# A vision-tower kernel: fewer token groups projected in front of the software pipeline, more inside it, and the column means taken from the scaled gains

## The reference, cut to what matters

```
p = layernorm(patches) * g1 + b1            # over 768
h = layernorm(p @ W_tok) * g2 + b2          # 768 -> 192
q, k, v = h @ W_qkv                         # 8 heads of 24
attn = softmax(normalised(q)^T normalised(k) * temp)   # 24 x 24 per head and image
h1 = layernorm(h + (attn v) @ W_proj + b_proj)
out = layernorm(h1 + soft_moe(h1))          # 8 experts, 4 slots each
```

## Time and profile before

| quantity | value |
|---|---|
| median of 3 runs | 140.48 us (139.16 to 142.77) |
| the profiled execution | 140.0 us, span 138.0 us |
| TensorE busy | 115.0 us (83%) |
| VectorE busy | 88.9 us (64%) |
| ScalarE busy | 69.0 us (50%) |
| GpSimd busy | 67.0 us (49%) |
| bytes moved | 10.34 MB in 7677 packets |

### The profile page before, as it was taken

How to read it: one execution, slowest core, us unless ns; L and a number is a source line. 1 busy time by engine, 2 the same in 40 slices (tenths; PEclk the granted TensorE clock), 3 DMA queues, 4 the chain that set the end, 5 groups by cost and what they waited for, 6 DMA issues and landing times.

```text
span 138.0 us, 4819 instructions
## 1 busy us (share of the span) xinstructions
PE 115.0 (83%) x1779; PEld 93.6 (68%) x1779; DVE 88.9 (64%) x380; ACT 69.0 (50%) x234; POOL 67.0 (49%) x158
## 2 busy tenths in 40 slices
PE   0297799999699999999999999997986860999920
PEld 0297799888377868578787796866964630788700
DVE  0211999999643687985857558586987440159980
ACT  3000004242862848648675686846644468763553
POOL 8500277767847428837265382743664000007871
PEclk9999999999999999999999999999999555599995
DMA  1999899988000000000000000000000000000232
GB/s 14 337 293 278 269 305 320 314 319 214 5 7 0 5 0 7 5 0 7 0 5 5 0 5 0 10 5 0 5 0 7 0 0 0 5 0 24 72 89 71
DMA packets 7677, 10.34 MB, mean 75 GB/s; under 512 B 2056, under 2 KB 5032, under 8 KB 7656
## 3 DMA queue, kind: packets, MB, share of 16 engines
q1 hardware_dynamic: 7656, 10.06, 24.2%
HBM read 9.17 MB, written 0.88 MB: 73 GB/s over the span
## 4 chain that ended last, share of the span: by engine, by line
PE 47%; DVE 22%; issue 12%; POOL 10%; ACT 4%; DMA 3%; SPq 1%; POOLq 1%; DVEq 0%; ACTq 0%
DVE st L649 8%; PE ps L565 7%; PE ps L436 6%; PE ps L476 5%; PE ps L496 3%; PE ps L542 3%; PE ps L399 3%; DMA wt<-in_w_tok 3%; PE ps L489 3%; PE ps L519 3%; DVE y L663 3%; PE ps L578 3%; DVE st L671 2%; PE ps L507 2%; PE ps L407 2%
## 5 line engine op out<-in xcount | busy, mean ns | idle before, releaser
L417 PE MATMUL ps<-wc,xT 128*108 128x192 f32 (+1 forms) x132 | 23.0, 327 | 1.5 <-DVE wc L637 1.5
L940 ACT ACTIVATE hT<-ps,b,g 96x108 f32<-96x108 f32 (+1 forms) x22 | 8.4, 430 | 27.9 <-PE ps L426 27.9
L417 PEld LDWEIGHTS ps<-wc,xT 128*108 128x108 f32 (+1 forms) x132 | 20.7, 170 | 2.0 <-DVE wc L637 1.8
L436 PE MATMUL ps<-wqk,hT 96*108 96x384 f32 (+1 forms) x44 | 16.2, 490 | 0.7 <-ACT qp L962 0.7
L1125 POOL TENSOR_SCALAR pw<-mv 108x1 f32<-108x1 f32 (+1 forms) x11 | 3.7, 337 | 21.3 <-DVE mv L780 21.3
L476 PE MATMUL ps<-hT,wv 96*128 96x108 f32 (+1 forms) x88 | 12.5, 284 | 0.0
L1139 POOL TENSOR_SCALAR var<-mv 108x1 f32<-108x1 f32 (+1 forms) x11 | 2.4, 223 | 18.9 <-DVE mv L875 18.4
L950 ACT ACTIVATE sq<-ps 108x384 f32<-108x384 f32 (+1 forms) x11 | 5.4, 490 | 12.4 <-PE ps L436 12.4
L476 PEld LDWEIGHTS ps<-hT,wv 96*128 96x128 f32 x88 | 10.7, 191 | 0.7
L649 DVE BATCH_NORM_STATS2 st<-xs 108x6 f32<-108x384 f32 (+1 forms) x22 | 10.9, 540 | 0.2 <-issue 0.2
L960 ACT ACTIVATE km<-ps,imgsel 108x192 f32<-108x192 f32 (+1 forms) x32 | 11.0, 418 | 0.0
(11 more groups left out here) (106 smaller groups left out, 304.6 us busy)
## 6 DMA issues: line engine op xcount, KB each, us to landing
xT<-in_x_t SPq DMA_DIRECT2D x10, 324.0 KB, 7.0
xs<-in_x SPq DMA_DIRECT2D x10, 324.0 KB
out<-o SPq DMA_DIRECT2D x10, 81.0 KB
wt<-in_w_tok SPq DMA_DIRECT2D x1, 576.0 KB, 4.2
wqk<-in_w_qk SPq DMA_DIRECT2D x1, 288.0 KB, 8.7
xT<-in_x_t SPq DMA_DIRECT2D x1, 216.0 KB, 7.5
xs<-in_x SPq DMA_DIRECT2D x1, 216.0 KB
wv<-in_w_v SPq DMA_DIRECT2D x1, 192.0 KB, 9.0
```

The costliest lines, as they stand in the source:

```text
L417: mm = pe.matmul(tokp(g), xT[:, o + kc * n:o + (kc + 1) * n], wc[:, kc, :], start=kc == 0, stop=kc == KC - 1)
L436: mm = pe.matmul(qkp(g), hT[:, f, t0:t0 + tokens(g)], wqk[:, f, :, :, :].rearrange("p j h d -> p (j h d)"), start=f == 0, stop=f == 1)
L940: ins = act.activation(hT[:, f, t0:t0 + tokens(g)], htp(g)[:, f, :], ACT.Identity, bias=b2[:, f:f + 1], scale=g2[:, f:f + 1])
```

## The change

The column means are taken directly from the weight: the multiplier is now `gs1`, the gains divided by 768, instead of a constant, so they no longer wait for `wg`. `wg` and `share` disappear. `wc` is formed in six slices, and the first projection goes on slice by slice. `offset` moves behind the projection of group 0, and its copy on VectorE behind the statistics of group 0. The gains and the biases come in one transfer, the weight in two, laid out so that each partition's part is contiguous.

`P1` becomes 3: three groups are projected in front of the loop (their two later turns in steps 0 and 1), the others in steps 0 to 5: two each in steps 0 and 1, one each in 2 to 5. Their turns follow two steps later. The group's vector and GpSimd stages move with them. The slots' loads move in front of the x loads from group 4 on, `slot_sums` into VectorE's step 1, `slot_scale` to step 3. Group 10's projection uses bank 7. Unchanged parts and the moved norms on GpSimd are left out of this cut of the diff where the description says it all:

```diff
-P1 = 9
+P1 = 3
+TOKENS = {0: (3, 4), 1: (5, 6), 2: (7,), 3: (8,), 4: (9,), 5: (10,)}
+def late(stage, s, i):
+    groups = TOKENS.get(s, ())
+    if i < len(groups):
+        stage(groups[i])
+def turn_step(g):
+    return 2 + next((t for t, groups in TOKENS.items() if g in groups), g - P1 - 1)
+def turned(s):
+    return P1 + sum(len(TOKENS.get(t, ())) for t in range(s - 1))
...
-            return ps[0:tokens(g), 6 + g % 2, 0:D]
+            return ps[0:tokens(g), 6 + g % 2 if g < NG - 1 else 7, 0:D]
...
-            sp.dma_start(g1[:, :], ln1_g).then_inc(ln1_in, 16)
-            sp.dma_start(b1[:, :], ln1_b).then_inc(ln1_in, 16)
-            sp.dma_start(wt[:, :, :], w_tok.rearrange("(k p) e -> p k e", p=128)).then_inc(wtok_in, 16)
+            sp.dma_start(gb1[:, :, :].rearrange("p t k -> p (t k)"), ln1_gb).then_inc(ln1_in, 16)
+            for i in range(2):
+                k0 = i * KC // 2
+                sp.dma_start(wt[:, k0:k0 + KC // 2, :].rearrange("p k e -> p (k e)"),
+                             w_tok[:, k0 * D:(k0 + KC // 2) * D]).then_inc(wtok_in[i], 16)
...
+            def column_means():
+                pe.wait_ge(gs1_ready, 1)
+                for kc in range(KC):
+                    if kc % (KC // 2) == 0:
+                        pe.wait_ge(wtok_in[kc // (KC // 2)], 16)
+                    mm = pe.matmul(csp(), gs1[:, kc:kc + 1].broadcast_to([128, 128]), wt[:, kc, :],
+                                   start=kc == 0, stop=kc == KC - 1)
+                mm.then_inc(csp_ready, 1)
...
                 if g >= 2:
-                    pe.wait_ge(y1_ready, g - 1)
+                    pe.wait_ge(y1_ready, g - 1 if g < NG - 1 else g)
                 for kc in range(KC):
+                    if g == 0:
+                        pe.wait_ge(wc_ready, kc + 1)
...
             def turn_h(g):
                 pe.wait_ge(n_ready, g + 1)
+                if turn_step(g) > 4:
+                    pe.wait_ge(xnT_ready, turn_step(g) - 4)
...
-            offset()
             column_means()
-            pe.wait_ge(wc_ready, 1)
             for g in range(P1):
                 token(g)
+                if g == 0:
+                    offset()
...
-                at(turn_h, s + P1 - 2 - 1, P1 - 2)
-                at(token, s + P1 - 1, P1)
+                if s < P1 - 1:
+                    turn_h(s + 1)
+                late(turn_h, s - 2, 0)
+                late(token, s, 0)
                 at(gram, s - 1)
                 at(mix, s - 2)
+                late(turn_h, s - 2, 1)
                 at(turn_xn, s - 4)
                 at(slot_in, s - 6)
                 at(norms, s)
+                late(token, s, 1)
...
+                for kc in range(KC):
+                    dve.scalar_tensor_tensor(wc[:, kc, :], wt[:, kc, :], gb1[:, 0, kc:kc + 1], csp(),
+                                             ALU.mult, ALU.subtract).then_inc(wc_ready, 1)
...
+            mean_shares()
             token_weights()
             x_stats(0)
             x_moments(0)
+            token_offset()
...
+                late(x_stats, s + 1, 0)
                 at(max_c, s - 5)
+                late(token_stats, s - 1, 0)
                 at(unit_h1, s - 4)
                 at(max_d, s - 5)
+                late(token_moments, s - 1, 0)
                 at(scales, s - 1)
+                late(x_moments, s + 1, 0)
                 at(y_sums, s - 2)
                 at(scores, s - 1)
+                late(token_out, s, 0)
+                late(token_stats, s - 1, 1)
...
+                late(x_moments, s + 1, 1)
                 at(take_d, s - 5)
-                at(ln2_norm, s + P1 - 2, P1)
+                late(ln2_norm, s - 1, 0)
+                late(ln2_norm, s - 1, 1)
                 at(residual_moments, s - 2)
+                late(token_out, s, 1)
```

More of the change, by code:

```diff
@@ L62, in tokens, with build @@
     return images(g) * TOK
-def build(nc, x, x_t, w_tok, ln1_g, ln1_b, ln2_g, ln2_b, g2col, b2col, w_qk, w_v, w_proj, b_proj, temp, slots, scale,
+def build(nc, x, x_t, w_tok, ln1_gb, ln2_g, ln2_b, g2col, b2col, w_qk, w_v, w_proj, b_proj, temp, slots, scale,
           w_down, b_down, w_up, b_up, ident_h, imgsel_h, negmask_h, out):
@@ L78, in build @@
         negmask = sb("negmask", [128, GI * SL])
-        g1 = sb("g1", [128, KC])
-        b1 = sb("b1", [128, KC])
+        gb1 = sb("gb1", [128, 2, KC])
+        gs1 = sb("gs1", [128, KC])
         wt = sb("wt", [128, KC, D])
-        wg = sb("wg", [128, KC, D])
         wc = sb("wc", [128, KC, D])
         bw = sb("bw", [128, D])
-        share = sb("share", [128, 128])
         g2 = sb("g2", [F, 2])
@@ L242, in build @@
         ln1_in = sem("ln1_in")
-        wtok_in = sem("wtok_in")
+        wtok_in = [sem(f"wtok_in{i}") for i in range(2)]
         ln2_in = sem("ln2_in")
@@ L376, in _ @@
             sp.dma_start(scl[:, :], scale.broadcast_to([F, 1])).then_inc(slots_in, 16)
+            for g in range(4, NG):
+                load_x(g)
             sp.dma_start(wd[:, :, :, :].rearrange("p f n h -> p f (n h)"), w_down).then_inc(experts_in, 16)
@@ L394, in _ @@
         def _(pe):
+            def column_means():
[6 more added lines that the diff above has]
+                mm.then_inc(csp_ready, 1)
             def offset():
-                pe.wait_ge(ln1_in, 32)
-                pe.wait_ge(wtok_in, 16)
                 for kc in range(KC):
-                    mm = pe.matmul(bwp(), b1[:, kc:kc + 1].broadcast_to([128, 128]), wt[:, kc, :],
+                    mm = pe.matmul(bwp(), gb1[:, 1, kc:kc + 1].broadcast_to([128, 128]), wt[:, kc, :],
                                    start=kc == 0, stop=kc == KC - 1)
                 mm.then_inc(bwp_ready, 1)
[L403 to L408, removed]
             def token(g):
@@ L912, in _ @@
                 at(score_shift, s - 1)
+                late(token_moments, s - 1, 1)
                 at(scale_d, s - 5)
@@ L917, in _ @@
                 at(h1_inverse, s - 3)
+                late(x_stats, s + 1, 1)
                 at(residual, s - 2)
@@ L1048, in _ @@
                 at(take_c, s - 6)
-                at(take_h, s + P1 - 2 - 1, P1 - 2)
+                if s < P1 - 1:
+                    take_h(s + 1)
+                late(take_h, s - 2, 0)
                 at(take_qk, s)
                 at(norm_logs, s)
+                late(take_h, s - 2, 1)
                 at(exp_c, s - 5)
@@ L1067, in _ @@
         def _(pool):
-            pool.memset(share[:, :], 1.0 / PD).then_inc(share_set, 1)
             pool.memset(mhalf[:, :], -0.5).then_inc(cleared, 1)
@@ L1147, in _ @@
             for g in range(P1):
-                at(ln1_var, g + 1)
-                at(ln1_root, g + 1)
+                ln1_var(g + 1)
+                ln1_root(g + 1)
                 ln2_var(g)
                 ln2_root(g)
+            ln1_var(P1 + 1)
+            ln1_root(P1 + 1)
             pool.wait_ge(rows_in, 48)
@@ L1156, in _ @@
             for s in range(16):
[L1157 removed]
+                if s == 4:
                     pool.wait_ge(sp_sum, 1)
@@ L1161, in _ @@
                 at(keep_h_offset, s - 5)
+                for i in range(2):
+                    if s >= 3:
+                        late(ln1_var, s - 2, i)
+                        late(ln1_root, s - 2, i)
                 at(keep_h_gain, s - 2)
-                at(ln2_root, s + P1 - 5, P1)
-                at(ln1_root, s + P1 + 1 - 3, P1 + 1)
-                at(ln1_var, s + P1 + 1, P1 + 1)
-                at(ln2_var, s + P1 - 4, P1)
+                for i in range(2):
+                    late(ln2_var, s - 4, i)
+                    late(ln2_root, s - 4, i)
                 at(q_scale, s - 3)
```

43 lines of the change are left out of this document (17 added, 26 removed).

## The result

The changed kernel takes 143.38 us (median of 20, 141.15 to 146.54), the kernel before 140.9 us beside it (20 runs, 138.48 to 144.25). The ratio is 1.018, interval 1.013 to 1.023: slower, by 1.3 to 2.3 per cent. (Ratios in this text leave disturbed executions out on both sides, so they are not quotients of the medians.) The profiled execution took 141.89 us, span 139.8.

The account below looks back on a forecast made before the run. TensorE's queue was taken to bound the kernel to the end of step 7. Starting the loop 14.1 us earlier, less 11.7 given back and waits of 0.9 and 1.2, gains 0.3: profiled 139.7, median 140.2 us, range 137.5 to 142.8.

Parts of the forecast that it names:

- part 7: Loop: turn_h waits behind the vector engine's norm, with 0.5 to 0.7 us at turn_h(7); 0.9 us in all.
- Part 6: Loop steps 0 to 7 lengthen by the moved projections and turns: 53.0 us against 41.3 before, 11.7 given back.
- Part 8: Steps 6 and 7: ln2_norm stands behind take_d, so TensorE waits 0.6 us each time, 1.2 in all.
- Part 1: Front: weight in two halves, first half landed at 4.1 us instead of 5.83; the second half costs nothing.
- Part 5: Loop start after three groups: qk(0) at 20.15 instead of 34.28, 14.1 us earlier; constants have 0.65 us of cover.
- Part 4: Group 0, then offset: rate doubles 6 us after first matmul, at 10.2; group 0 ends at 11.7 (ends 10.9, 13.2).
- Rival B: Clock falls before the loop, between 15.8 and 20.15; loses 1.9 to 3 us, 142.1 to 143.2; chance 0.10.
- Parts 2, 3 and 9: Front: column means from the weight, done at 8.4; six slices, first projection at 9.0; remaining edits cost nothing.
- Rivals C and D: C: vector engine bounds the loop, 142.3 us, chance 0.08. D: whole weight's transfer gates both halves, 141.5, chance 0.07.

Follow-up runs that it names:

- f4: The kernel before, unchanged, run once more for a second profile; a single execution of 141.38 us.
- after: The changed kernel with the whole change, against the kernel before it; 143.38 us, ratio 1.018.
- f5: The changed kernel with the weight in one transfer and ln2_norm ahead of take_d; 139.71 us, ratio 0.997.
- e11: The kernel before with only its weight split into two transfers, matmuls waiting for both halves; ratio 1.036.
- f1: The changed kernel with the weight in one contiguous transfer instead of two; 139.28 us, ratio 0.999.
- before: The kernel without the change, the base of the ratios; 140.9 us beside the changed kernel.
- e3: The changed kernel with ln2_norm ahead of take_d in VectorE's list; 142.87 us, ratio 1.014.
- e4: The changed kernel loading only a quarter of each xs row from group 4 on; 141.46 us, ratio not determined.
- e5: The changed kernel with an unused pad of 32 bytes ahead of xs; ratio 1.034.
- e8: The changed kernel with the 32-byte pad, ln2_norm ahead of take_d, and five matmuls on a constant tile ahead of everything to warm TensorE; ratio 1.015.
- e9: The changed kernel with the weight's old rows of 768 bytes, still in two halves; ratio 1.025.
- e1: The kernel before with the new front alone, nine groups still in front of the loop; 144.88 us, ratio 1.033.
- e7: The changed kernel with the 32-byte pad ahead of xs and ln2_norm ahead of take_d; ratio 1.009.
- f6: The changed kernel with the weight's second half issued behind the x loads of slot 0; 142.6 us, ratio 1.023.
- f2: The old front with the new loop and ln2_norm ahead of take_d; 138.12 us, ratio 0.991.
- e12: The kernel before with the first norm's gains and biases in one transfer, 16 unused bytes behind; 143.14 us, ratio not determined.
- e2: The new loop (three groups in front) behind the old front; 139.98 us, ratio 0.994.

## Why the prediction was wrong

The forecast of the profiled execution was 139.7 us; it took 141.89. The 2.2 us are 1.65 at the front and 0.4 in the loop (55.56 measured, 53.0 + 0.9 + 1.2 = 55.1 forecast). That the loop came out so near is luck: 1.9 us of waiting for x, which I had at nothing, stood where the 0.9 of part 7 and 0.5 of parts 6 and 8 did not come. By part:

**Part 1, the weight in two halves, is the step that failed.** Its mechanism came true (4.29 against 4.2), and its price was written as a gain only: "it costs nothing". In ten profiles with the weight in one transfer the x row takes 147.6 to 171.2 ns; in nine with its halves back to back, 180.6 to 193.5. The two ranges don't overlap, but those of a part of the rows do: the first 528 rows took 188.5 ns in f4 and 186.8 in after, and the others 174.4 in f5 and 170.3 in e11. The split alone costs 3.6% in the old kernel (e11), and without it the changed kernel is at 0.999 (f1). I had given a transfer only a landing time of its own and never asked what it does to the transfers behind it, although some 20 us of loads stand there. The path from the split to the lost time is shown in part only: 1.9 us of it in after's loop, and the constants below.

**Part 5, the 3 us or more for each x load, and the 0.65 us of cover for the constants.** Both rested on transfer times of before. The x load took 10.4 us to land, not 7.0, and 1.9 us of it reached TensorE (55.56 less 53.67). The constants landed at 11.48 + 9.5 = 21.0, not at 19.5. In the profiled execution they did not decide, since TensorE was later still; in e3, e4, e5, e8 and e9 they did, and qk(0) waited 3.07 to 4.48 us where hT alone takes 1.0. With the weight in one transfer the first profile of before has wp at 19.5, but f5 at 20.64, f4 at 21.3 and f1 at 21.7: the 0.65 us of cover was too little for that variation even without the split. For the first half itself, 3.1 us from issue to landing was measured, 2.9 forecast.

**Part 4, the doubling of the rate.** I took it 6 us after the first matmul and bounded group 0 by 13.2. The bound's bad end is what the profiled execution showed, 1.5 of the 1.65 us; f1, without the split, shows it too, so this is not the split's work. In e1, e3, e4, e5, e9 and f5 the rate doubled before the first projection, at 7.7 to 8.9, and in after, e7, f1 and f6 at 13.9 to 14.3. So the moment varies between executions, and I had one execution to read it from. But this term could not have saved the forecast: in the profiles where the front was fast the constants held qk(0), with the split to 21.29 (e4) at the earliest and without it to 20.82 (f5), where I had 20.15. The Trainium skill, "TensorE: Matmul & The Clock Gate", Part 1, states that the number of slow matmuls at the start differs from run to run of one kernel; the traces agree, and I had not used it.

**Rival B, the clock falls before the loop, had a chance of 0.10 and happened in part.** Its place was right (e3, e8: in the idle stretch before qk(0)) and its price was put at 1.9 to 3 us; step 0 to qk(1) grew by 3.24 us in e3 and by 1.7 in f5 and f6. I had looked for it in the latencies of the norm; in e3 and e8 it came in a wait for a transfer. It is not rare. Of the seven profiles with the split in front of the new loop, five show a granted clock of 0.50 that begins between 19.4 and 22.5 and lasts 3.4 us (e4) or 6.8 us (e3, e5, e8, e9); after and e7 show none. How often it strikes after itself can only be inferred, from the mean granted clock of each execution, which is 0.909 to 0.916 in the four profiles with 6.8 us: it is at most 0.916 in 13 of 20 (and in all six of e5, whose 1.034 is the worst of the kernels with the new loop), with a median of 143.68 us, and 0.939 or more in the other seven, with 141.69. In the 42 executions of the four kernels with the new loop and one transfer it is never below 0.927. That is 2 us that the profiled execution does not show, and the greater part of the median's distance from it (143.38 against 141.89, where I had put 0.5). The mean also holds the falls near the end, whose length varies, and f5's profile has a fall in front at a mean of 0.943, so the count is a rough one.

**Part 6, the steps' lengths, held:** 53.67 less the two waits is 52.6, forecast 53.0. **Part 8 held to 0.1 us:** 0.55 and 0.54, forecast 0.6 each; the exchange of two lines gives 1.07 back (f2). **Part 7 did not appear:** steps 3 and 4 of after show no such wait; the only one of its kind, 1.52 in step 2, came from an x load. So my tie between the two queues was a lead of the vector engine's. **Parts 2, 3 and 9** came as forecast. **Rivals C and D** did not occur: the loop is TensorE's, and the halves gate separately.

So the forecast "0.3 us faster" lies within what the loop part does by itself (0.987 to 1.0005), by coincidence, as it counted a gain of the front; and the front is what loses.

What stays open is why two transfers of the weight back to back slow the rows that come much later. It is not the alignment, not the length of rows, not the number of transfers ahead, and with the halves apart the row was 169.3 ns, in one profile, at a time no better. The row is also not a switch: among the kernels with one transfer it reaches 171.2, and e12 waited for x at 170.8. e12's own ratio is unsettled too, so that the merged gains and biases cost nothing is shown only together with the new loop (f1, 0.999).

## What to carry to other kernels

A transfer that is split to start earlier has a price outside itself: compare the rate of everything behind it, not only its landing. Before shortening a front, list what else must have landed when it ends, with landing times and not only with issue times, and ask what the engine's clock does if it must stand there: e3 and e8 had their first turn 2.7 and 3.0 us earlier than after, and started the loop no earlier, and then at half rate. When a change has two parts, cost and run them apart; here one was worth about 0.6%, with two lines exchanged 0.9%, and the other lost 3.3%. And profile the kernel before more than once: two profiles of it here differ by 3.3 us at step 8 (75.56 and 78.91), more than the change is worth.

## What the runs showed of the hardware

The weight of 576 KB in two transfers instead of one took the mean time of later 3072-byte rows from 148 to 171 ns (ten profiles) up to 181 to 194 ns (nine profiles), and the old kernel's time up by 3.6%. Placing the row's target 32 bytes off changed no time (0.997). At the start the page's granted clock reads full while records of 192 columns take 0.35 us instead of 0.17, and the moment at which that ends varies: after a first matmul at 4.3 to 4.4 it came at 7.8 in e1 and at 13.9 in after. Six profiles have TensorE standing idle for 1.7 to 4.5 us in front of qk(0) (f5, e4, e3, e9, e5, e8). In each the granted clock fell to 0.50, at 19.4 to 22.5, for 3.4 us in f5 and e4 and 6.8 in the others. With 1.0 us of idle time there was no fall in after, e2, e7, f1 and f2, and one of 3.4 us in f6. Near the end the granted clock falls in every profile, for 6.8 us in some and for 10.2, 13.7 or 17.1 in others.
